# A causal attention block on one core: key loads of 512 positions in a ring of eight instead of 1024 in a ring of four

## The reference

```
h   = layernorm(x)                                        # no gain, no bias
qkv = h @ w_attn.T + b_attn + 0.5 * (h @ la.T @ lb.T)     # 16 heads of 16
att = softmax(causal(q k^T / 4)) v                        # 4096 x 4096 per head
p   = lora_linear(att, w_proj, b_proj, la_proj, lb_proj)
x   = x + layernorm(p)
h   = layernorm(x)
for blk in 0, 1, 2:                                       # weights of 4 bit with scales per 16, plus LoRA
    y = gelu(layernorm(linear(h)) * gamma + beta);  h = linear(y) + h
out = x + layernorm(h)
```

## Time and profile before

| | us |
|---|---|
| median of 3 runs (lowest, highest) | 1344.06 (1343.75, 1345.02) |
| the profiled execution's own time | 1344.06 |
| its span | 1342.3 |
| TensorE busy | 1277.7 (95%) |
| ScalarE busy | 1174.9 (88%) |
| VectorE busy | 626.3 (47%) |
| GpSimd busy | 163.1 (12%) |
| SyncE waiting for scores (line 1102) | 456.3 |

### The profile page before, as it was taken

The page is one execution under the profiler, slowest core; times in us unless marked ns, Lnnn a source line. Parts: engine busy times, 40 slices in busy tenths (PEclk is TensorE's granted clock), DMA queues, the critical chain, the costliest instruction groups (busy, mean ns, idle before and its releaser), DMA issues.

```text
span 1342.3 us, 30945 instructions
## 1 busy us (share of the span) xinstructions
PE 1277.7 (95%) x11725; PEld 537.5 (40%) x11725; DVE 626.3 (47%) x2226; ACT 1174.9 (88%) x1401; POOL 163.1 (12%) x503
## 2 busy tenths in 40 slices
PE   8998899999999999999999999999999999999856
PEld 6554433333333333333333433333333333333345
DVE  6774265446643364335632373334632373333066
ACT  4665779999999999999999999999999999999733
POOL 3211311101111010000000000000000010100053
PEclk9998989999999999999999999999999999999979
DMA  5984975476663566565654654455536473631000
GB/s 178 303 269 146 144 167 106 103 106 124 101 86 67 95 103 97 82 102 95 98 86 63 98 100 60 72 97 98 98 58 90 79 116 52 92 58 30 5 1 16
DMA packets 76500, 132.29 MB, mean 99 GB/s; under 512 B 21926, under 2 KB 37308, under 8 KB 76348
## 3 DMA queue, kind: packets, MB, share of 16 engines
q1 hardware_dynamic: 72060, 126.01, 51.5%
q10 hardware_dynamic: 4288, 4.26, 1.0%
HBM read 105.03 MB, written 20.97 MB: 94 GB/s over the span
## 4 chain that ended last, share of the span: by engine, by line
PE 69%; ACT 10%; issue 4%; DVE 3%; SPq 2%; POOL 1%; DMA 1%; ACTq 0%; DVEq 0%
PE O L1255 30%; PE S L1240 23%; PE F L204 13%; ACT probs L1183 5%; PE F L1301 2%; ACT L1199 2%; SPq L588 2%; ACT L1183 2%; ACT feed_mem L1199 1%; DMA attT<-o_div 1%; SPq L1083 1%; DVE stC L1342 1%; PE S L1320 1%; DVE mvC L1345 0%; DVE tmpC L1348 0%
## 5 line engine op out<-in xcount | busy, mean ns | idle before, releaser
L1183 ACT ACTIVATE probs<-S 128x1024 f32<-128x1024 f32 (+3 forms) x1152 | 997.9, 967 | 68.3 <-PE S L1240 52.3
L1255 PE MATMUL O<-probs,vg 128*32 128x512 f32 (+3 forms) x4608 | 533.8, 565 | 3.1 <-DVE o_turned L1385 2.2
L1240 PE MATMUL S<-q_op,k_op 64*128 64x512 f32 (+3 forms) x2304 | 403.8, 430 | 19.5 <-ACT probs L1183 12.0
L1240 PEld LDWEIGHTS S<-q_op,k_op 64*128 64x128 f32 x2304 | 184.4, 185 | 404.7 <-ACT probs L1183 329.4
L1162 POOL TENSOR_SCALAR_AFFINE_SELECT probs<-probs 128x256 f32<-128x256 f32 x256 | 105.4, 420 | 1020.3 <-ACT probs L1183 1015.9
L1255 PEld LDWEIGHTS O<-probs,vg 128*32 128x32 f32 x4608 | 113.9, 109 | 192.8 <-issue 163.9
L1414 DVE TENSOR_TENSOR feed_mem<-F,bffn 128x512 f32<-128x512 f32 x56 | 38.6, 689 | 218.4 <-PE F L204 218.4
L204 PE MATMUL F<-wfT,feed_mem 128*32 128x256 f32 x1792 | 117.6, 384 | 0.0
L1420 DVE SCALAR_TENSOR_TENSOR feed_mem<-F,cols,feed_mem 128x256 f32<-128x256 f32 (+1 forms) x58 | 25.1, 474 | 154.6 <-PE F L204 154.6
L1385 DVE STREAM_TRANSPOSE o_turned<-O 128x512 f32<-128x512 f32 x32 | 22.9, 716 | 111.5 <-PE O L1255 110.8
L1342 DVE BATCH_NORM_STATS2 stC<-feed_mem 128x6 f32<-128x256 f32 x172 | 64.7, 416 | 13.0 <-DVEq L1376 12.2
(11 more groups left out here) (169 smaller groups left out, 889.0 us busy)
## 6 DMA issues: line engine op xcount, KB each, us to landing
k_op<-qk_rows SPq DMA_DIRECT2D x512, 128.0 KB, 4.9
qk_rows<-parts SPq DMA_DIRECT2D x32, 512.0 KB, 4.9
q_op<-qk_rows SPq DMA_DIRECT2D x256, 64.0 KB, 4.6
k_op<-qk_rows SPq DMA_DIRECT2D x128, 64.0 KB, 2.4
x_in<-in_L_attn_x ACTq DMA_DIRECT2D x8, 512.0 KB, 5.6
feed_mem<-in_L_attn_x SPq DMA_DIRECT2D x16, 256.0 KB, 3.4
attT<-o_div SPq DMA_DIRECT2D x126, 32.0 KB, 2.4
out<-feed_mem SPq DMA_DIRECT2D x14, 256.0 KB, 3.8
```

Of the source, the lines that this page charges most:

```text
L1183: nc.scalar.activation(probs[:, n % NP, :, 0:TT - q0], S[:, n % NS, :, 0:TT - q0], ACT.Exp, scale=SCALE).then_inc(exp_ok, 1)
L1240: last = nc.tensor.matmul(S[:, n % NS, a, 0:TT - q0], k_op[mine, c % RING, n % 2, k0:k0 + P], q_op[mine, v % QS, n % 2, q0:TT], start=True ...
L1255: last = nc.tensor.matmul(O[h * STRIP:(h + 1) * STRIP, q0:TT], vg[:, kb, col:col + STRIP], probs[:, (2 * b + h // 2) % NP, h % 2, 0:TT - q ...
```

## The change

The ring of keys has eight slots of 512 positions, where it had four of 1024. A key load brings 512 positions (the table `CHUNKS`), so there are 144 of them instead of 80, each of eight DMAs of 64 KB; before, most were of eight times 128 KB. Eight key loads are issued early instead of four, and all early loads begin one tile sooner. The three groups of late weight loads are one tile earlier as well. Several smaller edits come with it: the bias of v lies again in the last columns of `qkv_mem` (`bv`), whose zero fills go; the zero fills of `la` move from the start of `project` to the last but one tile; the statistics of x stand before the second split of a tile, not the third; dequantising is spread evenly over tiles 1 to 6; the load of x for tile 2 is issued in `project`, not at the end of `prepare_weights`; ScalarE's last copy of `lbT_late` waits for the last values; SyncE waits for all stores at the end of `project`, not in `guard`; and the planner's clock of TensorE starts at 0, not at 0.15 us.

```diff
-RING, QS = 4, 3
-EARLY_AT = {3: [("k", 0), ("q", 0)], 4: [("k", 1), ("q", 1)], 5: [("k", 2), ("q", 2)], 6: [("k", 3)]}
+RING, QS = 8, 3
+EARLY_AT = {2: [("k", 0), ("q", 0)], 3: [("k", 1), ("q", 1)], 4: [("k", 2), ("q", 2)], 5: [("k", 3), ("k", 4)],
+            6: [("k", 5), ("k", 6)], 7: [("k", 7)]}
...
@@ prepare_weights, ScalarE
                         copy_turned(act, nc, g, 0, 0)
-                        act.dma_start(g["x_in"][:, 0, :, :], x_tiles[2]).then_inc(g["front"]["x_loaded"][0], 16)
...
@@ project, late_loads: n == 1, 2, 3 become
-            if n == 1:
+            if n == 0:
...
@@ project, SyncE
                         if m < len(EARLY_AT.get(n, [])):
                             early_load(sp, EARLY_AT[n][m])
+                for m in range(4):
+                    sp.wait_ge(stored[m], COPIES * (1 + NT))
                 sp.wait_ge(w["small_in"], 16 * 2)
...
@@ project, ScalarE
-                    if 1 <= n < NT - 2:
+                    if n + 2 < NT:
...
                 act.wait_ge(w["lbT_turned"], 4)
+                act.wait_ge(v_out, NT + 1)
...
@@ project, VectorE
-                for half in (slice(R, 2 * R), slice(2 * R, P)):
-                    nc.vector.memset(w["la"][half, 1:, :], 0.0).then_inc(w["la_filled"], 1)
-                    nc.vector.memset(g["qkv_mem"][half, NC * 3 * C:], 0.0).then_inc(w["lbT_filled"], 1)
...
-                        if m == 2 and n + 2 < NT:
+                        if m == 1 and n + 2 < NT:
...
-                    for m in range(2 * BLK):
-                        if n == min(m + 2, NT - 2):
-                            dequantise(m)
+                    if 1 <= n <= 2 * BLK:
+                        dequantise(n - 1)
+                    if n == NT - 2:
+                        for half in (slice(R, 2 * R), slice(2 * R, P)):
+                            nc.vector.memset(w["la"][half, 1:, :], 0.0).then_inc(w["la_filled"], 1)
...
@@ guard, SyncE
-                for m in range(4):
-                    sp.wait_ge(g["stored"][m], STORES)
...
@@ the tables of attention
-KEYS = [(v, max(s - 1, 0), min(s + 1, 2)) for v, (t, i) in enumerate(VISITS) for s in range(t, -1, -2)]
+CHUNKS = [(v, s) for v, (t, i) in enumerate(VISITS) for s in range(t, -1, -1)]
...
@@ plan
-    for c in range(len(KEYS)):
-        item(("k_load", c), "SP", 3.6 if c >= EARLY_K else 0.0, [("score", 2 * KEYS_END[c - RING] + 1) if c >= RING else None], KEYS_START[c] - 12)
+    for c, (v, s) in enumerate(CHUNKS):
+        item(("k_load", c), "SP", 3.6 if c >= EARLY_K else 0.0, [("score", 2 * CHUNK_END[c - RING] + 1) if c >= RING else None], CHUNK_END[c] - 16)
...
-    free["PE"] = HOP
...
@@ attend_and_feed, SyncE
-                            load_rows(sp, d, k_op[:, c % RING, :, 0:n * TT], 1, VISITS[v][1], slice(low * TT, (low + n) * TT), k_in[c % RING], LOW + need)
+                            load_rows(sp, d, k_op[:, c % RING, :, :], 1, VISITS[v][1], slice(s * TT, (s + 1) * TT), k_in[c % RING], LOW + need)
```

More of the change, by code:

```diff
@@ L50 @@
 LOAD = 16 * 2 * PRODUCTS
-COPIES = 16
-STORES = COPIES * (1 + NT)
 EPS = 1e-5
@@ L338, in project @@
         x_loaded, held, rstd, nmr, rstd_ok = (g["front"][n] for n in ("x_loaded", "heldA", "rstd", "nmr", "rstd_ok"))
-        stored = g["stored"]
+        stored = [sem(f"stored{m}") for m in range(4)]
         norm_ok, turned, xT_ok = (g["front"][n] for n in ("norm_ok", "turned", "xT_ok"))
@@ L347, in project @@
         SLOTS, BANKS = 2, 4
+        COPIES = 16
         w = g["raw"]
@@ L588, in load_rows, with renew_rows @@
             eng.dma_start(dst[row:row + D].bitcast(F32), src[0, a][:, :, tok]).then_inc(done, 16)
-def renew_rows(eng, d, dst, which, g, done):
+def renew_rows(eng, d, dst, which, g, part, done):
     src = d["rows"][which, EXTRA].rearrange("(g p a e) t -> g a e p t", g=NG, p=PAIRS, a=2)[g]
@@ L596, in renew_rows @@
         row = a * HALF + (PRODUCTS - 1) * D
-        eng.dma_start(dst[row:row + D].bitcast(F32), src[a][:, :, 0:TT]).then_inc(done, 16)
+        eng.dma_start(dst[row:row + D].bitcast(F32), src[a][:, :, part * TT:(part + 1) * TT]).then_inc(done, 16)
 def guard(nc, g, d):
     QB = T // P
-    SPAN = 4 * TT
-    chunks = [(b, k) for b in range(QB) for k in range(0, (b + 1) * P, SPAN)]
+    KEYS = 4 * TT
+    chunks = [(b, k) for b in range(QB) for k in range(0, (b + 1) * P, KEYS)]
     NCH = len(chunks)
@@ L726, in _ @@
                                 end = (b + 1) * P
-                                for k0 in range(k, min(k + SPAN, end), TT):
+                                for k0 in range(k, min(k + KEYS, end), TT):
                                     w = min(TT, end - k0)
@@ L744 @@
 VISITS = [(t, i) for t in range(NT) for i in range(NG)]
-KEYS = [(v, max(s - 1, 0), min(s + 1, 2)) for v, (t, i) in enumerate(VISITS) for s in range(t, -1, -2)]
+CHUNKS = [(v, s) for v, (t, i) in enumerate(VISITS) for s in range(t, -1, -1)]
 BLOCKS = [(v, t, c, s * NB + b, b * P if s == t else 0)
-          for c, (v, low, n) in enumerate(KEYS) for t in (VISITS[v][0],) for s in range(low + n - 1, low - 1, -1) for b in range(NB)]
+          for c, (v, s) in enumerate(CHUNKS) for t in (VISITS[v][0],) for b in range(NB)]
 NBLK = len(BLOCKS)
 LAST = {v: n for n, (v, _, _, _, _) in enumerate(BLOCKS)}
-KEYS_START = {c: n for n, (_, _, c, _, _) in reversed(list(enumerate(BLOCKS)))}
-KEYS_END = {c: n for n, (_, _, c, _, _) in enumerate(BLOCKS)}
+CHUNK_END = {c: n for n, (_, _, c, _, _) in enumerate(BLOCKS)}
 DIAG = [n for n, (_, t, _, kb, _) in enumerate(BLOCKS) if kb >= t * NB]
@@ L1456, in build @@
         g["wqkvT"] = g["qkv_mem"][:, 0:NC * 3 * C].rearrange("p (c o) -> p c o", c=NC)
-        g["k_op"], g["q_op"] = sb("k_op", [P, RING, PAIRS, 2 * TT], F32R), sb("q_op", [P, QS, PAIRS, TT], F32R)
-        g["stored"] = [ctx.enter_context(nc.semaphore(f"row_stored{m}")) for m in range(4)]
+        g["bv"] = g["qkv_mem"][:, NC * 3 * C:]
+        g["k_op"], g["q_op"] = sb("k_op", [P, RING, PAIRS, TT], F32R), sb("q_op", [P, QS, PAIRS, TT], F32R)
         g["k_in"] = [ctx.enter_context(nc.semaphore(f"k_in{s}")) for s in range(RING)]
@@ L1462, in build @@
             g["x_in"] = early.enter_context(nc.sbuf_tensor("x_in", [P, 2, NB, C], F32))
-            g["bv"] = early.enter_context(nc.sbuf_tensor("bv", [P, C], F32))
             g["front"], g["raw"] = x_front(early, nc), weight_buffers(early, nc, g)
```

30 lines of the change are left out of this document (15 added, 15 removed).

## The result

The changed kernel takes 1357.32 us (median of 4 runs, 1354.3 to 1359.84), the kernel before 1343.9 us on the same chip (4 runs, 1342.32 to 1345.02): 1.0089 times as long, interval 1.0073 to 1.0104. The direction was forecast and the size was not: 13.4 us are lost by these medians, where 6.5 were forecast, and the time lies above the range. The four runs scatter more than those of the other kernels. Twenty-one executions of the changed kernel are on record, from 1353.6 to 1359.8 us with a median of 1355.3 and a mean of 1355.7; the ratio fits their mean, and it is a loss of 12.0 us. The scatter goes with the granted clock: 0.984 in the fastest execution, 0.980 in the slowest. The profiled execution took 1355.51 us, its span is 1353.8 (before 1342.3).

What follows compares the result with a forecast made beforehand. TensorE was taken to set the projection, then a 5.6 us handover, then ScalarE's exponentials to pace attention except at its beginning. Sum: 1344.06 + 5.8 (projection) + 0.7 (start of attention) = 1350.6, forecast 1350.5 us, range 1344.5 to 1354.5.

Steps and rivals of the forecast that it cites:

- the x statistics: Projection, VectorE: statistics ahead of the second split; if x of tile 2 is late TensorE waits in tile 1, cost 0.
- SyncE's lag: Projection: early loads in six tiles put SyncE 5.25 us behind, so the last store is issued at about 116.0.
- the front with x in time: Projection's end: last store lands at 119.3 where VectorE ended at 113.54 before; term +5.8 us, bounds +0.6 to +8.9.
- the start of attention: Attention's first scores: a fold step before the first score, a third ahead of the eighth; term +0.7 us.
- The landing in line with the handover: Projection's end: SyncE waits 3.3 us for the last store's landing, then the 5.6 us handover follows.
- The stall, the middle, the tail: Attention: first-projection stall again 7 to 9 us; 60 more key loads fit SyncE's spare time, 0; tail 0.
- SyncE keeps up: Rival, projection: lag does not build, front costs only +0.6 to +2, total 1345.7 us; chance 0.20.
- the middle is bound: Rival, attention from 174.1 to 309: loads of 6.64 us make SyncE the bound, +2, total 1352.6 us; chance 0.05.
- The lag reaches TensorE: Rival, tile 6 or 7: VectorE's store stall nears 6 us and delays TensorE by 3, total 1353.5 us; chance 0.13.
- Faster: Rival, start of attention: half the key bytes shorten issues, last move 5.1 us sooner, total 1340.3 us; chance 0.10.
- The memsets: Tile 6, VectorE: two memsets before tile 7's first split, net under +3.1 us there, nothing added to the sum.
- A rule weighed: Key DMAs: skill's coalescing rule says halving relieves nothing; the trace shows 2.4 us landing for 64 KB, 4.9 for 128 KB.

Runs made afterwards that it cites:

- u_stats: Changed kernel with the statistics of x back before the third split of a tile, not the second; 1351.05 us, 1.0064 of the kernel before.
- u_x2: Changed kernel with the load of x for tile 2 back at the end of the weight preparation, ahead of the weights; 1350.72 us, 1.0056 of before.
- u_late: Changed kernel with only the late weight loads (w_late, lb, la) put back one tile later; 1354.1 us, 1.0072 of the kernel before.
- u_front: Changed kernel with most front edits undone; ring of eight, early table and planner as changed; 1351.54 us, 1.0058 of the kernel before.
- u_hop: Changed kernel with the planner's TensorE starting at HOP again, so three scores stand ahead of the first fold; 1351.8 us, 1.0062 of before.
- ring8: u_front with the early table of early4 and the planner line of u_hop, meant to leave only the ring of eight; 1348.27 us, 1.0034 of before.
- b_sp: Kernel before with the planner's SyncE times raised: load 4.4 instead of 3.6, move 2.5 instead of 1.8; 1336.24 us, 0.9947 of before.
- b_feed36: Kernel before with the plan's due times for projection and feed-forward work at 36.0, step 74.6, instead of 26.0 and 76.0; 1347.02 us, 1.0024 of before.
- u_best: u_front with the planner lines of u_hop and b_sp, keeping ring of eight and early table; 1340.32 us, 0.9979 of the kernel before.
- u_wait: Changed kernel with SyncE's wait for all stores back in the guard, behind the projection's barrier; 1351.29 us, 1.0059 of the kernel before.
- early4: Changed kernel with the early table of before (seven loads from tile 3, four key pieces), ring still eight; 1352.9 us, 1.0071 of before.
- u_memset: Changed kernel with the two memsets of la back at the start of the projection; 1355.45 us, 1.0085 of the kernel before.

## Why the prediction was wrong

**The step that failed** is that on the x statistics: "If it is late, TensorE waits in tile 1. Cost taken as 0, since SyncE's lag absorbs a later TensorE." I had named the event and priced it at nothing. It landed 7.2 us later than before (25.3 against 18.1), and TensorE lost 4.06 us: 2.54 of waiting and 1.53 of lower clock. They were not absorbed, since SyncE's loads and stores are interleaved with the tiles: its lag is counted in a tile's own time and stands on top of a tile that comes late. Against u_stats, where TensorE is in time, SyncE's first key load starts 4.2 us later (49.38 and 45.22), its last one 4.5 (112.41 and 107.90), and the last store 5.5 (118.8 and 113.3), of which 1.0 is that last load itself (5.40 and 4.38 us to issue). The price of the term put at 0 was 5.8 us at the first exponential (131.9 and 126.1) and 3.4 to 5.5 in time. u_stats, u_x2 and u_late show the cause from three sides; the prediction held both parts (statistics ahead of the split, x beside 1.5 MB) and left them in two sentences. The trace of before had the price as well: there the same 1.5 MB took 9.2 us to land. x beside it from 16.25 lands at 25.4, and the second split with TensorE behind it follows by the queue of VectorE.

**The sum, in the forecast's terms.** First exp 11.95 us late = 4.3 + 1.87 + 5.8: the front with x in time (u_stats; forecast 5.8), the start of attention (forecast 0.7), and x (forecast 0). That the first two add up to 6.2, near the 6.5 forecast, is luck: one was put too high and the other too low, by 1.5 and 1.2.

**The same sum by u_front** is 3.24 + 4.6 + 2.2 + 1.87. 3.24 is u_front's first instruction against before, with the wait behind the barrier: VectorE, which waited 3.87 us for a store's landing in tile 7, ends 1.70 us later (115.24 and 113.54), and that is the early loads' part; ScalarE's copy, which now waits for it, ends 0.88 behind; and from there to the first instruction it takes 6.26 us instead of 5.60. 4.6 is the last store's later issue (118.8 - 114.2): x, and what of the front is with it; 2.2 is the wait's place (10.4 - 8.2); 1.87 the longer way from first instruction to first exp (2.70 - 0.83).

**SyncE's lag: right in kind, too large.** Key loads start at 49.38, 62.20, 74.33, 87.52, 100.16 and 112.41: 12.82, 12.13, 13.19, 12.64 and 12.25 apart, 3.9 us over five tiles of 11.82, where I had 5.25; the gaps do not rise. With x on time (u_stats) the last store is issued at 113.3, not 116.0, and the first instruction comes at 123.43, not 125. The forecast's +5.8 would have been +4.3 by itself.

**The landing in line with the handover: right in kind, too small.** SyncE waited 3.7 us for it, and the last store landed 4.6 us after its issue, where I had 3.3. The handover from the landing (123.5) took 5.7, near the 5.6 forecast. Moved back, the wait gives 2.3.

**The start of attention: too small.** 1.87 us at the first exp for a fold put at 1.8, and of it little came back: my reason for +0.7 (the fourth exponential had stood behind both steps) shows in the second visit, 9.9 late instead of 11.95, but the order of feed work takes it again by the tenth (12.3). I had looked at the first eight scores and not at the order behind them. u_hop puts the planner's line at 2.4 us by spans and 3.6 by ratios.

**The stall, the middle, the tail.** 7.45 us of stall (7 to 9 forecast). SyncE waited 258.1 us for scores instead of 456.3, near the 230 forecast, and bound nothing. The tail was 1.3 us shorter, not 0.

**Rivals.** "SyncE keeps up" and "the middle is bound" fell. "The lag reaches TensorE" did not happen as told: VectorE waited 3.42 us for a store in tile 6, and TensorE kept 11.82 a tile there. "Faster" fell for the kernel as it is: with half the bytes per key load the seven loads and four moves still took 41.1 us of SyncE (137.69 to 178.8), not 37.6, where 42.7 had been. The memsets cost nothing that can be told, as in the forecast's sum. ScalarE's wait for the last values was put at nothing beyond the barrier; where SyncE does not hold that barrier (ring8) it costs 0.7 us. The gaps between the eleven groups of the earlier trace rows are ten, with the same 2 us.

**A rule weighed, again.** The median landing of a 64 KB key DMA is 2.3 us after the change, against 4.9 for 128 KB, and no time was won by it. The size of the DMA alone does not set it: the query loads were of 64 KB in both kernels, and their landing fell as well. Before and after:

```profile
q_op<-qk_rows SPq DMA_DIRECT2D x256, 64.0 KB, 4.6
```
```profile
q_op<-qk_rows SPq DMA_DIRECT2D x256, 64.0 KB, 2.3
```

It is 2.3 or 2.4 us in every kernel with the ring of eight, and 4.6 and 5.0 in b_sp and b_feed36 with the ring of four. Why is not shown. The Trainium skill, in "DMA: Bandwidth & Descriptors", section "Rules for kernel authors", asks to coalesce small transfers. u_best against b_sp agrees only weakly: the kernel with the small loads takes 4.8 us more by spans, but that is its later start, which the number of issues ahead of attention sets and not the size of a transfer.

## What to carry to other kernels

A wait that moves ahead of another engine's input in an in-order queue is to be priced as if it came late, and "absorbed" is no price: a delay upstream and a delay downstream add where the second is counted in the first's tiles. Where an order comes from a planner, compare its durations with the trace before turning its knobs: it had 3.6 and 1.8 us for SyncE's groups that took 3.7 to 4.9 and 2.4 up to the fourth move, and 4.4 and 2.5 in their place gained 6.4 us, where the ring gained nothing. An experiment that undoes a part of a change should be read against the diff: one small wait that stayed in ring8 was most of its delay at the front. A wait for landings belongs behind the barrier that the landings don't need.

## What the runs showed of the hardware

TensorE's tile 1 took 8.66 us in the changed kernel and 7.13 in u_wait, for the same 16 matmuls. Windows of the two kernels, ahead of the tile and in it (after the colon PE, PEld, DVE, ACT, POOL busy, then the granted clock):

```profile
28.20:31.10 2.90, 0.41 (x5) 0.11 (x5) 2.50 (x5) 2.17 (x3) 2.49 (x6) 0.95 0.48 124
31.10:39.70 8.60, 8.60 (x17) 3.67 (x18) 5.74 (x21) 4.61 (x9) 1.42 (x6) 0.82 1.03 325
```
```profile
28.10:30.80 2.70, 0.40 (x4) 0.10 (x4) 2.30 (x5) 2.17 (x3) 2.28 (x6) 1.00 0.51 131
30.80:37.90 7.10, 7.09 (x17) 3.03 (x18) 5.76 (x21) 4.62 (x9) 1.44 (x6) 1.00 1.06 321
```

TensorE was busy 0.41 of 2.90 us in the one and 0.40 of 2.70 in the other; the first was granted 0.82 in the tile (part of it at 1.2 GHz), the second stayed at 2.4 GHz. So 1.53 of the 4.06 us lost are clock. The other kernels with the late x and the early statistics agree with the first: the two waits of TensorE ahead of tile 1 add up to 2.34 us in u_wait, and to 2.54, 2.65, 2.68 and 2.70 in changed, early4, u_hop and u_memset, where the tile took 8.66, 8.73, 8.69 and 8.83. Whether the length of the wait decides, or its place in time, is not shown by five executions.

The same load of 0.5 MB, on a queue of its own (ScalarE's), landed 3.9 us after its issue with no weight load beside it (before and u_late), 9.1 beside 1.5 MB of weights, and 11.6 beside 1.1 MB of weights and a group of key loads. Separate queues did not keep them apart.
